# Turning the gathered slot rows with transposing transfers on SyncE's queue instead of on TensorE

## The chip, the cores and the metric

The kernel runs on one core of one Trainium2 chip. Its time is the device time of one execution in microseconds (us). Lower is better.

## What is computed

The reference is one layer of a vision tower: 32 images are cut into 36 patches each, embedded to 256 numbers, a class token is put in front (37 tokens for each image, 1184 in all), then attention with a memory, then a mixture of experts. Only the last part meets the change:

```python
shared = jnp.einsum('th,hd->td', jax.nn.silu(x_flat @ shared_w1.T), shared_w2.T)
gate_logits = x_flat @ gate_w.T
top_k_gates, top_k_idx = jax.lax.top_k(gate_logits, TOP_K)      # TOP_K = 2 of 8 experts
top_k_gates = jax.nn.softmax(top_k_gates, axis=1)
h = jnp.einsum('td,ehd->teh', x_flat, experts_w1)               # 256 -> 1024
expert_out = jnp.einsum('teh,edh->ted', jax.nn.silu(h), experts_w2)   # 1024 -> 256
selected = jnp.einsum('ted,te->td', expert_out, gates)
out = shared + selected
```

## The kernel before

The order of the work on each engine is written out by hand; semaphores tie the engines together. There are three stages.

The front (up to about 125 us) embeds, normalizes and attends, 11 tiles of 111 tokens. It writes each normalized token as a row of 512 fp16 numbers (a high and a low part of 256 numbers) to a DRAM tensor, `x_rows`.

The shared expert (about 125 to 186 us) goes over ten units of 119 tokens, `shared_up` and `shared_down`. Beside it the routing is worked out: which token goes to which slot.

The slots (from 185.7 us) are 26 tiles of 128 tokens, each of one expert. For slot j, GpSimd gathers 128 rows of `x_rows` into `slot_rows[:, j % 4]` (`gather`). TensorE turns them in four 128x128 pieces into bank 4 (`rows_of`, `turn`, L539). ScalarE copies the bank to `x_t[:, j % 2]` (`copy_x_t`, L953). Then TensorE does step j (`slot_step`): eight chunks, and in each the six matmuls of the first layer of slot j (L733, `up_chunk`) and two of the second layer of slot j - 1 (L746 and L748, `down_chunk`). After chunk 4 of step j it turns the rows of slot j + 1. Step 0 (`first_slot`) does the same with the last shared unit. ScalarE applies silu to each half of a slot (L902), VectorE makes the low part (L1238) and scales the result (L1419, L1422), and GpSimd adds the 128 result rows to the output in DRAM (L1116), one such transfer at a time.

SyncE's queue brings the weights of the experts: 36 chunks of 512 KB, `load_chunk`, L350, into a ring of six stage buffers. ScalarE and VectorE split each chunk into a high and a low half (L866, L1244). A load of chunk c waits until chunk c - 6 is split:

```python
def load_chunk(c):
    last = c - STAGES
    if last >= 0:
        wait_split(sp, last + 1)
    sp.dma_start(stage[:, c % STAGES], w_rows(c)).then_inc(stage_in[c % STAGES], 16)
```

VectorE splits chunks 18 to 21 just as step 0 begins, and two chunks in each of the steps 1 to 7 (`late_lo`). SyncE does nothing else after chunk 13: `for c in range(FRONT_CHUNKS, NCHUNK): load_chunk(c)`, with FRONT_CHUNKS = 13 and NCHUNK = 36.

## Time and profile before

| | us |
|---|---|
| median of 3 runs | 349.19 (349.02 to 349.57) |
| the profiled execution, its own time | 350.72 |
| its span | 348.8 |
| TensorE busy | 316.5 (91% of the span) |
| VectorE busy | 225.8 |
| ScalarE busy | 181.8 |
| GpSimd busy | 154.1 |

The span is the stretch from the first to the last instruction of the profiled execution. Busy time is the sum of an engine's own instructions. The stages bind differently, so the rows below are read by stage, in microseconds from the span's start.

### The profile page before, as it was taken

To read this page: it belongs to the slowest core of one execution; us is meant where nothing else is said; L and a number is where in the kernel's file an instruction comes from. 1 tells how busy PE (TensorE), PEld (TensorE's weight loads), DVE (VectorE), ACT (ScalarE), POOL (GpSimd) and SP (SyncE) were. 2 spreads that over 40 slices of the span, in tenths; PEclk is the share of its full clock that TensorE was granted. 3 is DMA by queue.
4 is the path that set the end of the run, shared out by engine and by line. 5 is a ranking of instruction groups with operands and counts; after the bars stand their busy time and mean duration, and the time that the engine had idled before them with its cause. 6 is when DMAs were issued, how large, how long until landed. Compare 5 with 4: busy or idle time off the path is not lost.

```text
span 348.8 us, 9611 instructions
## 1 busy us (share of the span) xinstructions
PE 316.5 (91%) x3366; PEld 267.9 (77%) x3366; DVE 225.8 (65%) x510; ACT 181.8 (52%) x395; POOL 154.1 (44%) x224
## 2 busy tenths in 40 slices
PE   3789899999998989999999999999999999999960
PEld 2668788877787889899999777777787777777750
DVE  0235678889888677569988687765656555554540
ACT  1136557877677575655767878763233232323210
POOL 0525557667774341510153235455435353543321
PEclk9989999999999899999999999999999999999995
DMA  7461235437300000293379878333232332323121
GB/s 260 144 212 41 99 104 157 128 114 271 106 20 26 17 25 29 59 333 90 78 179 246 311 192 251 61 60 55 44 62 36 58 46 49 48 46 48 17 32 15
DMA packets 18324, 36.36 MB, mean 104 GB/s; under 512 B 3269, under 2 KB 10920, under 8 KB 18280
## 3 DMA queue, kind: packets, MB, share of 16 engines
q1 hardware_dynamic: 11848, 27.71, 24.5%
q0 software_dynamic: 6432, 8.03, 14.7%
q8 instruction: 31, 0.51, 0.6%
q14 instruction: 13, 0.11, 0.1%
HBM read 28.52 MB, written 7.21 MB: 102 GB/s over the span
## 4 chain that ended last, share of the span: by engine, by line
PE 74%; DVE 10%; ACT 5%; issue 4%; DMA 2%; POOL 2%; SPq 0%; DVEq 0%; ACTq 0%; POOLq 0%
PE bank L733 20%; PE bank L746 14%; PE bank L460 8%; PE bank L748 6%; PE bank L485 6%; PE bank L591 6%; PE bank L550 5%; DVE weights L1244 2%; PE bank L539 2%; PE bank L493 1%; PE bank L417 1%; DMA weights<-in_w_embed 1%; DVE weights L1185 1%; DMA out_rows<-y,add_id 1%; PE bank L437 1%
## 5 line engine op out<-in xcount | busy, mean ns | idle before, releaser
L733 PEld LDWEIGHTS bank<-x_t,weights 128*128 x1248 | 87.2, 98 | 25.7
L733 PE MATMUL bank<-x_t,weights 128*128 128x128 f16 x1248 | 103.4, 219 | 0.0
L902 ACT ACTIVATE act_out<-bank 128x512 f32<-128x512 f32 (+2 forms) x72 | 42.1, 585 | 88.4 <-PE bank L733 74.9
L746 PE MATMUL bank<-weights,hid_hi 128*128 x200 | 76.1, 382 | 0.3
L1116 POOL DMA_INDIRECT out_rows<-y,add_id x26 | 42.6, 1637 | 71.0 <-DVE y L1422 53.8
L1238 DVE SCALAR_TENSOR_TENSOR hid_lo<-act_out,hid_hi 128x512 f16<-128x512 f32 (+2 forms) x72 | 48.6, 680 | 13.9 <-ACT hid_hi L913 12.5
L748 PE MATMUL bank<-weights,hid_lo 128*128 x200 | 54.5, 273 | 0.0
L1244 DVE SCALAR_TENSOR_TENSOR weights<-stage,weights 128x1024 f16<-128x1024 f32 x36 | 42.7, 1221 | 0.4 <-ACT weights L866 0.2
L460 PE MATMUL bank<-weights 128*111 128x256 f32 x132 | 32.5, 399 | 7.2 <-DMA weights<-in_w_embed 5.7
L866 ACT ACTIVATE weights<-stage 128x1024 f16<-128x1024 f32 x36 | 36.2, 1047 | 0.0
L460 PEld LDWEIGHTS bank<-weights 128*111 128x111 f32 x132 | 23.6, 184 | 13.3 <-DMA weights<-in_w_embed 5.7
L1083 POOL DMA_INDIRECT slot_rows<-x_rows,gather_id x26 | 27.3, 1051 | 13.2 <-DMA out_rows<-y 5.5
L1043 POOL TENSOR_SCALAR weights<-weights 111x1 f32<-111x1 f32 x22 | 6.4, 292 | 55.9 <-DVE weights L1142 55.8
L1419 DVE TENSOR_SCALAR y<-bank,slot_gate 128x256 f32<-128x256 f32 x25 | 12.1, 482 | 26.1 <-PE bank L748 24.6
L550 PE MATMUL bank<-x_t,weights 128*128 128x119 f16 (+1 forms) x480 | 27.6, 216 | 0.0
L591 PE MATMUL bank<-weights,hid_hi 128*119 128x256 f16 (+1 forms) x160 | 27.3, 273 | 0.2 <-DVE hid_lo L1238 0.2
L550 PEld LDWEIGHTS bank<-x_t,weights 128*128 128x128 f16 x480 | 26.2, 98 | 0.2
L1236 DVE TENSOR_SCALAR hid_hi<-act_out 128x512 f16<-128x512 f32 x36 | 15.4, 426 | 16.7 <-ACT act_out L902 14.6
L485 PEld LDWEIGHTS bank<-weights 128*128 128x128 f32 x176 | 23.7, 212 | 1.4 <-ACT weights L820 0.6
L485 PE MATMUL bank<-weights 128*128 128x111 f32 x176 | 24.4, 298 | 0.4 <-ACT weights L820 0.4
L1102 POOL DMA_DIRECT2D out_rows<-y x10 | 8.9, 890 | 33.7 <-DVE y L1436 28.9
L746 PEld LDWEIGHTS bank<-weights,hid_hi 128*128 128x128 f16 x200 | 19.3, 96 | 5.2 <-issue 1.4
(138 smaller groups left out, 544.8 us busy)
## 6 DMA issues: line engine op xcount, KB each, us to landing
stage<-in_w_ffn SPq DMA_DIRECT2D x36, 512.0 KB
weights<-in_patches SPq DMA_DIRECT2D x11, 333.0 KB, 3.0
x_rows<-rows SPq DMA_DIRECT2D x11, 111.0 KB
out_rows<-weights SPq DMA_DIRECT2D x10, 111.0 KB
out_rows<-y POOLq DMA_DIRECT2D x9, 119.0 KB, 6.1
weights<-in_w_embed SPq DMA_DIRECT2D x1, 768.0 KB, 4.4
weights<-in_w_qk SPq DMA_DIRECT2D x1, 512.0 KB, 6.2
slot_rows<-x_rows,gather_id POOLq DMA_INDIRECT x26, 3.8
```

The costliest lines, as they stand in the source:

```text
L460: mm = nc.tensor.matmul(embed_bank(t), s_patch[:, t % 2, k], s_we[:, k], start=(k == 0), stop=(k == PC - 1))
L485: mm = nc.tensor.matmul(bank[5][:, o * T:(o + 1) * T], s_wqk[:, k, o], xln_t[:, t % 2, k], start=(k == 0), stop=(k == KC - 1))
L550: mm = nc.tensor.matmul(o, weights[:, bass.ds(base + 2 * k * CHUNK + 2 * (col - col % D) + w * D + col % D, P)], x_of(2 * x + k), start=(k ...
L591: mm = nc.tensor.matmul(bank[down_bank(n)][0:m, 0:D], hid[:, n % 2, c * P:c * P + m], weights[:, at + w * D:at + (w + 1) * D], start=(c == ...
L733: mm = nc.tensor.matmul(o, weights[:, bass.ds(base + 2 * k * CHUNK + 2 * (col - col % D) + w * D + col % D, P)], x_t[:, b, (2 * x + k) * P ...
L746: nc.tensor.matmul(bank[5 + b][0:m, :], hid_hi[:, b, c * P:c * P + m], weights[:, bass.ds(at, 2 * D)], start=(c == 0), stop=False)
L748: mm = nc.tensor.matmul(bank[5 + b][0:m, 0:D], hid_lo[:, b, c * P:c * P + m], weights[:, bass.ds(at, D)], start=False, stop=(c == HC - 1))
L866: nc.scalar.mul(hi_of(c), staged_of(c), W_SCALE).then_inc(w_hi, 1)
L902: nc.scalar.activation(d_, s_, ACT.Silu, scale=1.0 / (X_SCALE * W_SCALE)).then_inc(hid_acted, 1)
L1116: nc.gpsimd.indirect_dma_start(out=out, out_offset=bass.IndirectOffsetOnAxis(ap=add_id[:, j:j + 1], axis=0), in_=y[:, j % 2], in_offset=No ...
L1238: nc.vector.scalar_tensor_tensor(out=four(hid_lo), in0=src, scalar=H_SCALE, in1=four(hid_hi), op0=ALU.mult, op1=ALU.subtract).then_inc(lo_ ...
L1244: nc.vector.scalar_tensor_tensor(out=lo_of(c), in0=staged_of(c), scalar=W_SCALE, in1=hi_of(c), op0=ALU.mult, op1=ALU.subtract).then_inc(w_ ...
```

## The change

The turns on TensorE (L539) and the copies on ScalarE (L953) are taken out, and bank 4 isn't used for them any more. In their place SyncE's queue carries four transposing transfers for each slot, each 128x128 fp16 from `slot_rows` to `x_t`, both in SBUF. A turn of slot j waits for the gather of slot j and, from slot 2 on, until the first layer of slot j - 2 is through, since `x_t` has two buffers. The weight transfers up to chunk 25 stand ahead of the turns of slots 0 and 1; the last ten stand two by two ahead of the turns of slots 2 to 6. TensorE waits at the head of step j for the four transfers of slot j. GpSimd's gather of slot j + 4 waits for them too, where it waited for the turn on TensorE.

```diff
+AHEAD = 26
-        x_turned = sem("x_turned")
-        x_t_ready = sem("x_t_ready")
+        x_t_in = [sem(f"x_t_in{i}") for i in range(2)]
-            for c in range(FRONT_CHUNKS, NCHUNK):
+            def turn_slot(j):
+
+                sp.wait_ge(slot_rows_in[j % 4], 16 * (j // 4 + 1))
+                if j >= 2:
+                    sp.wait_ge(hid_ready, 2 * (UNITS + j) - 2)
+                for q in range(4):
+                    sp.dma_start(x_t[:, j % 2, q * P:(q + 1) * P], slot_rows[:, j % 4, q * P:(q + 1) * P],
+                                 transpose=True).then_inc(x_t_in[j % 2], 16)
+
+            for c in range(FRONT_CHUNKS, AHEAD):
                 load_chunk(c)
+            turn_slot(0)
+            turn_slot(1)
+            for j in range(2, SLOT_TILES):
+                for c in range(AHEAD + 2 * (j - 2), min(AHEAD + 2 * (j - 1), NCHUNK)):
+                    load_chunk(c)
+                turn_slot(j)
...
             shared_down(UNITS - 2, 0)
-            rows_of(0)
             shared_down(UNITS - 2, 1)
...
-                pe.wait_ge(x_t_ready, j + 1)
+                pe.wait_ge(x_t_in[b], 4 * 16 * (j // 2 + 1))
                 for c in range(HC):
                     up_chunk(n, b, P, this_expert, c)
                     if c == 4 and j + 1 < SLOT_TILES:
-                        rows_of(j + 1)
                         know(j + 1)
...
-            def copy_x_t(j):
-                act.wait_ge(x_turned, j + 1)
-                act.wait_ge(hid_ready, 2 * (UNITS + j) - 2)
-                v_ = bank[4][:].bitcast(F16)[:, 0:4 * P]
-                nc.scalar.copy(x_t[:, j % 2], v_).then_inc(x_t_ready, 1)
...
                 if j >= 4:
-                    pool.wait_ge(x_turned, j - 3)
+                    pool.wait_ge(x_t_in[j % 2], 4 * 16 * ((j - 4) // 2 + 1))
```

SyncE's queue at its end, before. L391 and L393 store results of the front; the 23 transfers of L350 are the weight chunks 13 to 35:

```order
57 L393 DMA x_rows<-rows 111x512
58 L391 DMA out_rows<-weights 74x256
59 L393 DMA x_rows<-rows 111x512
60 L350 DMA stage<-in_w_ffn 128x1024 x23
61 L60 UNCONDITIONAL_BRANCH
```

The same queue in the changed kernel, where L402 is the transposing transfer:

```order
60 L350 DMA stage<-in_w_ffn 128x1024 x13
61 L402 DMA_TRANSPOSE x_t<-slot_rows 128x128 x8
62 L350 DMA stage<-in_w_ffn 128x1024 x2
63 L402 DMA_TRANSPOSE x_t<-slot_rows 128x128 x4
64 L350 DMA stage<-in_w_ffn 128x1024 x2
65 L402 DMA_TRANSPOSE x_t<-slot_rows 128x128 x4
66 L350 DMA stage<-in_w_ffn 128x1024 x2
67 L402 DMA_TRANSPOSE x_t<-slot_rows 128x128 x4
68 L350 DMA stage<-in_w_ffn 128x1024 x2
69 L402 DMA_TRANSPOSE x_t<-slot_rows 128x128 x4
70 L350 DMA stage<-in_w_ffn 128x1024 x2
71 L402 DMA_TRANSPOSE x_t<-slot_rows 128x128 x80
```

So the turns of the first two slots stand behind thirteen weight chunks (13 to 25), and 104 transfers have joined the queue.

TensorE before, at the end of the last-but-one shared unit (L591 is its second layer) and the start of step 0 (L709 reads an expert's number, the ISA rows set addresses):

```order
304 L591 MATMUL bank<-weights,hid_hi 119x256 x2
305 L591 MATMUL bank<-weights,hid_lo 119x256
306 L539 MATMUL bank<-id,slot_rows 128x128 x4
307 L591 MATMUL bank<-weights,hid_hi 119x256 x2
308 L591 MATMUL bank<-weights,hid_lo 119x256
...
315 L709 TENSOR_LOAD expert_of x2
316 L733 ISA
317 L733 MATMUL bank<-x_t,weights 128x128 x2
```

The same place of the changed kernel, where L591 has become L599 and L733 has become L734:

```order
310 L599 MATMUL bank<-weights,hid_hi 119x256 x2
311 L599 MATMUL bank<-weights,hid_lo 119x256
312 L599 MATMUL bank<-weights,hid_hi 119x256 x2
313 L599 MATMUL bank<-weights,hid_lo 119x256
314 L717 TENSOR_LOAD expert_of x2
315 L734 ISA
316 L734 MATMUL bank<-x_t,weights 128x128 x2
```

The four turning matmuls are gone here, as they are in each step, and step 0 follows directly on the shared unit; its first instruction now waits on SyncE's transfers.

## Rows read from the trace of the kernel before

**Rows 1.** The page: busy time by engine, and the chain that ended last by engine.
```profile
PE 316.5 (91%) x3366; PEld 267.9 (77%) x3366; DVE 225.8 (65%) x510; ACT 181.8 (52%) x395; POOL 154.1 (44%) x224
PE 74%; DVE 10%; ACT 5%; issue 4%; DMA 2%; POOL 2%; SPq 0%; DVEq 0%; ACTq 0%; POOLq 0%
```

**Rows 2.** Windows: stretch, then busy us and instructions by engine, PEclk, DMA share, GB/s.
```profile
200.00:232.00 32.00, 31.76 (x377) 24.69 (x376) 25.26 (x35) 25.51 (x39) 14.98 (x12) 1.00 0.57 147
232.00:330.00 98.00, 98.00 (x1180) 77.61 (x1178) 54.12 (x106) 31.34 (x53) 44.06 (x35) 1.00 0.31 48
```

**Rows 3.** Waits from 186 to 332 us: who waited for whom, us, times, longest.
```profile
ACT act_out L902 <- PE bank L733: 70.2, 44, 2.4
```

**Rows 4.** TensorE's timeline in the late steps: start us, us, line, output and input.
```profile
280.18 0.50 PE L733 MATMUL bank<-x_t,weights 128*128 128x128 f16 x6
280.51 0.39 PE L539 MATMUL bank<-id,slot_rows 128*128 128x128 f16 x4
...
281.17 0.50 PE L733 MATMUL bank<-x_t,weights 128*128 128x128 f16 x6
...
282.49 0.50 PE L733 MATMUL bank<-x_t,weights 128*128 128x128 f16 x6
...
283.15 0.50 PE L733 MATMUL bank<-x_t,weights 128*128 128x128 f16 x6
...
286.19 0.39 PE L539 MATMUL bank<-id,slot_rows 128*128 128x128 f16 x4
```

**Rows 5.** TensorE's timeline at the first matmuls of step 0.
```profile
185.73 0.33 PE L733 MATMUL bank<-x_t,weights 128*128 128x128 f16 x3
```

**Rows 6.** SyncE's queue: issues of the weight chunks 24, 25, 30 and 31.
```profile
187.59 0.33 SPq L350 DMA_DIRECT2D stage<-in_w_ffn  x1
...
188.73 0.33 SPq L350 DMA_DIRECT2D stage<-in_w_ffn  x1
...
200.62 0.33 SPq L350 DMA_DIRECT2D stage<-in_w_ffn  x1
...
201.75 0.33 SPq L350 DMA_DIRECT2D stage<-in_w_ffn  x1
```

**Rows 7.** VectorE's timeline: the low halves of chunks 18 to 21.
```profile
186.35 4.62 DVE L1244 SCALAR_TENSOR_TENSOR weights<-stage,weights 128x1024 f16<-128x1024 f32 x4
```

**Rows 8.** Windows around the start of step 0, columns as in the second group.
```profile
188.00:200.00 12.00, 11.96 (x148) 9.78 (x146) 8.96 (x11) 9.37 (x14) 2.01 (x2) 1.00 0.94 294
188.00:193.00 5.00, 4.96 (x68) 4.47 (x66) 4.46 (x6) 3.63 (x6) 0.46 (x1) 1.00 0.94 248
```

**Rows 9.** DMA issues: count, KB each, median us from issue to landing.
```profile
stage<-in_w_ffn SPq DMA_DIRECT2D x36, 512.0 KB
...
slot_rows<-x_rows,gather_id POOLq DMA_INDIRECT x26, 3.8
out_rows<-y,add_id POOLq DMA_INDIRECT x26, 3.8
...
out_rows<-y SPq DMA_DIRECT2D x1, 128.0 KB, 2.3
```

**Rows 10.** Windows near the start and at the end, where TensorE has been idle.
```profile
16.00:18.00 2.00, 2.00 (x12) 2.00 (x11) 0.00 (x0) 0.60 (x1) 0.81 (x2) 0.50 0.45 107
...
338.00:340.00 2.00, 0.00 (x0) 0.00 (x0) 0.17 (x1) 0.00 (x0) 0.50 (x1) 1.00 0.09 12
340.00:349.00 9.00, 0.00 (x0) 0.00 (x0) 0.00 (x0) 0.00 (x0) 1.05 (x1) 0.50 0.14 15
```

**Rows 11.** The chain: the same 20 matmuls of a tile at half clock and later.
```profile
15.28 3.30 PE bank L485 x16
18.57 1.25 PE bank L493 x4
...
27.95 1.77 PE bank L485 x16
29.71 0.88 PE bank L493 x4
```

**Rows 12.** GpSimd's timeline: gathers and adds of slots.
```profile
205.05 1.00 POOL L1083 DMA_INDIRECT slot_rows<-x_rows,gather_id  x1 [0.30 <-issue]
208.99 1.60 POOL L1116 DMA_INDIRECT out_rows<-y,add_id  x1 [2.94 <-DMA out_rows<-y,add_id]
...
215.00 1.58 POOL L1116 DMA_INDIRECT out_rows<-y,add_id  x1 [3.12 <-DMA out_rows<-y,add_id]
...
235.91 1.58 POOL L1116 DMA_INDIRECT out_rows<-y,add_id  x1 [1.61 <-DVE y L1422]
...
240.46 1.58 POOL L1116 DMA_INDIRECT out_rows<-y,add_id  x1 [1.67 <-DMA out_rows<-y,add_id]
```

**Rows 13.** ScalarE's timeline: silu of the second half of slots 1, 2 and 3.
```profile
197.12 0.60 ACT L902 ACTIVATE act_out<-bank 128x512 f32<-128x512 f32 x1 [1.20 <-PE bank L733]
...
203.01 0.60 ACT L902 ACTIVATE act_out<-bank 128x512 f32<-128x512 f32 x1 [1.12 <-PE bank L733]
...
208.83 0.60 ACT L902 ACTIVATE act_out<-bank 128x512 f32<-128x512 f32 x1 [1.05 <-PE bank L733]
```

More of the change, by code:

```diff
@@ L534, in logits @@
                 mm.then_inc(logits_ready, 1)
-            def turn(src):
-                for q in range(4):
-                    mm = nc.tensor.transpose(bank[4][:].bitcast(F16)[:, q * P:(q + 1) * P],
-                                             src[:, q * P:(q + 1) * P], id16[:])
-                mm.then_inc(x_turned, 1)
             def up_half(n, half_, m, base, x_of):
@@ L712, in know @@
                                                       "expert_of is written")[1][0]
-            def rows_of(j):
-                pe.wait_ge(slot_rows_in[j % 4], 16 * (j // 4 + 1))
-                if j == 0:
-                    pe.wait_ge(h2_ready, NT)
-                turn(slot_rows[:, j % 4])
             shared_down(UNITS - 2, 0)
-            rows_of(0)
             shared_down(UNITS - 2, 1)
@@ L756, in first_slot @@
                 n = UNITS
-                pe.wait_ge(x_t_ready, 1)
+                pe.wait_ge(x_t_in[0], 4 * 16)
                 for c in range(HC):
                     up_chunk(n, 0, P, base_of[0], c)
-                    if c == 5:
-                        rows_of(1)
                     if c % 4 == 0:
@@ L788, in last_slot @@
                 n, b = UNITS + j, j % 2
-                pe.wait_ge(x_t_ready, j + 1)
+                pe.wait_ge(x_t_in[b], 4 * 16 * (j // 2 + 1))
                 for c in range(HC):
@@ L1012, in _ @@
                     late_hi(n)
-            copy_x_t(0)
             late_hi(UNITS - 1)
@@ L1019, in _ @@
                     hidden_hi(UNITS + j, 0)
-                copy_x_t(j + 1)
                 silu_half(UNITS + j, P, 1)
```

## Prediction

> **What bounds the kernel now.** I read the busy times first, to see which engine could bound: TensorE, busy 91% of the span and 74% of the chain that ended last [rows 1]. An average hides stages, so the windows come next. From 200 to 330 us, where the slots are, TensorE is busy 31.76 of 32 us and 98.00 of 98 us, at full clock (PEclk 1.00), while the DMA engines are at 0.57 and 0.31 [rows 2]. The waits show the other side of it: ScalarE waited 70.2 us in the slot stage for TensorE's first layer and TensorE for nobody worth naming [rows 3]. So in the slots any time taken off TensorE's own row of matmuls is gained, and any wait put at the head of a step is paid in full.
>
> TensorE's timeline of a late step gives the size of a step. From turn to turn it is 286.19 - 280.51 = 5.68 us. The chunk with the turn takes 281.17 - 280.18 = 0.99 us, one without 283.15 - 282.49 = 0.66 us, so a turn (four matmuls, L539) costs 0.33 us of TensorE [rows 4]. Without it a step is 5.35 us.
>
> **The change, part by part.**
>
> *Turns and copies removed.* 26 turns and 26 copies go. The turn of slot 0 lies before step 0, and what it gives is swallowed by the wait below; the other 25 give 25 x 0.33 = -8.25 us. The copies on ScalarE give nothing: that engine waits for TensorE anyway [rows 3].
>
> *Where the first turns stand.* This is the term that decides. SyncE issues the transfers of slot 0 only after the load of chunk 25, and that load waits until chunk 19 is split. In the trace chunks 24 and 25 are issued at 187.59 and 188.73 us [rows 6], because VectorE splits chunks 18 to 21 in one stretch from 186.35 us [rows 7]. TensorE wants slot 0 at 185.73 us [rows 5]. Nothing in the change moves these splits forward by more than the 0.3 us of the removed turn. So the first transposing transfer is issued at 188.73 + 0.33 = 189.1 us, 3.3 us after TensorE stands waiting for it. Behind the waiting instruction on TensorE stands all of steps 0 to 25 and the last shared unit.
>
> The DMA engines are full then: share 0.94 from 188 to 200 us, 294 GB/s, that is 3.53 MB [rows 8]. In that stretch chunks 26 to 29 (4 x 0.52 MB = 2.1 MB [rows 9]) and the last parts of the shared adds (some 0.3 MB) move. What is left, about 1.1 MB, is chunks 24 and 25. At 188 us they still lie ahead nearly whole; at 248 GB/s over 188 to 193 us (1.24 MB [rows 8]) they are through at about 193.0 us. The transfers of slot 0 lie behind them on the same queue. To that I add the 2.3 us to landing of SyncE's only other transfer out of SBUF, 128 KB [rows 9]: slot 0 is ready at 195.3 us. The wait is 195.3 - 185.73 = +9.6 us. Lower bound: the transfers overtake the weights, and land 3 x 0.33 + 2.3 = 3.3 us after 189.1, at 192.4 us: +6.7 us. Upper bound, by the gathers' 3.8 us to landing and 1.0 us of issue each [rows 9, 12]: 193.0 + 3 x 1.0 + 3.8 = 199.8 us: +14.1 us.
>
> *Clock after that wait.* At the end TensorE has no matmul from 338 us on; its clock is still 1.00 in the window to 340 us and 0.50, the 1.2 GHz level, in the nine us after it. Near the start, from 16 us, it works at 0.50 [rows 10], and there the same twenty matmuls take 3.30 + 1.25 us instead of 1.77 + 0.88 [rows 11]: +1.9 us. A wait of 9.6 us is long enough for the clock to fall, by the end of the kernel. I take +1.9 us; bounds 0 and 3.8 (twice that).
>
> *The later turns, weights gone.* The turn of slot j can begin when the first layer of slot j - 2 is through. That is the end of the eighth chunk's L733, 282.49 + 0.50 = 282.99 us, 0.16 us before the next step begins at 283.15 [rows 4]. It has to be done one step later: 5.35 + 0.16 = 5.5 us are there. I call L the time from that release to the landing of the fourth transfer. If L is over 5.5 us, step j and step j - 2 form a loop and each step costs (L - 5.5)/2 more, 24 times (slots 2 to 25). The trace has no transposing transfer. Lower bound 3.3 us (above); upper bound 3 x 1.0 + 3.8 = 6.8 us by the gathers, which are small-row transfers like these [rows 9, 12]: 24 x 0.65 = +15.6 us. I take L = 4.5 us, nearer to the lower end, since the queue and the fp16 tile are SyncE's and nothing has to be generated row by row on GpSimd. It is hidden by the step: 0. If that cover goes, each us over 5.5 costs 12 us.
>
> The Trainium skill, VectorE: DVE Perf Modes, The three transpose paths, gives 1309 ns for a 128x128 bf16 transpose by DMA and 390 ns on TensorE. Its DMA figure, four times one behind another, would be an estimate of 5.2 us and, with the first issue ahead, just about L = 5.5: still nearly nothing, but no cover left. The Trainium skill, Advanced Engine Details and Errata, X-Bar Transpose (TRN2), says that such transfers are as fast as regular ones, which would leave L at the lower bound. No row here shows either.
>
> *The turns among the weights.* In before, chunks 30 and 31 are issued 3.5 and 4.6 us after the end of step 1 (197.1 us [rows 6, 13]) and need 1.05 MB / 300 GB/s = 3.5 us on top of about 1 us; they are through at about 205.2 us, 2.2 us after the end of step 2 at 203.0 us [rows 13]. The turns of slots 3 to 6 are issued behind such a pair. L is 4.5 + 2.2 = 6.7 us there, (6.7 - 5.5)/2 = 0.6 us for each of four steps: +2.4 us. The gather of slot 5 is issued at 205.05 us and lands 3.8 us later, at 208.9 us, just when its turn could begin (end of step 3, 208.8 us [rows 12, 13]). With adds 6.0 us apart here (208.99 and 215.00 us [rows 12]) against steps of 5.5, slots 5 to 8 lose some tenths: +0.6 us. Together +3.0 us; bounds 0 (L = 3.3 us) and 7 (L = 6.8 + 2.2 = 9.0 us).
>
> *Issues on SyncE.* 104 more, each some 0.33 us if like a load [rows 6]: 1.3 us of a step of 5.35 on a queue that has little else to do there. Counted in L. The weight loads behind a turn wait for a split that comes later than the turn's release, so they aren't late.
>
> **The sum.** -8.25 + 9.6 + 1.9 + 0 + 3.0 = +6.25 us. On the profiled execution (350.72 us, span 348.8) that is 357.0 us; on the median of the runs, which is 1.5 us under it, 349.19 + 6.25 = **355.4 us**.
>
> **Rivals.**
>
> *The transfers don't fit into a step* (L over 5.5 us, chance 0.30). For it: small rows on shared DMA engines, 3.8 us to landing for one gather. Against it: the DMA share is only 0.31 [rows 2]. L = 6 to 7 us gives +6 to +18 us on the sum, and the first wait grows with it: 361 to 376 us.
>
> *Slightly faster* (chance 0.07). The mechanism is the first wait alone: slot 0's transfers don't lie behind chunks 24 and 25 but overtake them, and land at 192.4 us. With no cost of the clock and none among the weights the sum is -8.25 + 6.7 = -1.6: 347.6 us. It turns at a landing of slot 0 at 194.0 us if nothing else costs anything, at 192.1 us if the clock falls. For it: nothing in the trace shows the order in which two transfers of one queue land; against it: both are on one queue, and the issue itself is 3.3 us late.
>
> *The adds become the bound* (chance 0.07). One add waits for the one before; the fastest pair in the trace is 240.46 - 235.91 = 4.55 us apart [rows 12], 0.8 us under the new step. If 104 more transfers slow their landing by 1.5 us, VectorE and so TensorE lose 0.7 us in some 17 steps, +12 us: 367 us. Against it: the share of 0.31 leaves room.
>
> **How the numbers follow.** The forecast, wait at step 0 and hidden afterwards, has a chance of 0.52 and its own range is 350.5 to 360 us (first wait 6.7 to 14.1 us, the others between their bounds). With the rivals' 0.30, 0.07 and 0.07 and 0.04 for a sum near zero, 8 times in 10 it lies from 350.5 to 372 us. A difference of 0.2% (0.7 us) is about what can be told from none. Faster 0.07, within 0.04, slower 0.89.
>
> **What the changed profile would show.** No L539 or L953 and steps of 5.35 us from 240 us on, or longer with TensorE waiting for a DMA at each head of a step: that decides the second rival. A TensorE gap of some 9 us before the first L734, released by the transfer of slot 0, with PEclk 0.5 for some us after it. The first transposing transfer issued at about 189 us. Short waits in steps 3 to 8. I am wrong if the gap is under 7 us, if the transfers take more than a step, or if they hold the SyncE queue longer than a load does.

## The result and the profile after

The changed kernel takes 388.94 us in the median (386.57 to 393.02, four runs); the kernel before, run again beside it, 349.38 us (349.02 to 351.16). The ratio is 1.1098, interval 1.1021 to 1.1175: 11% slower, some 39 us. The prediction was 355.4 us with a range of 350.5 to 372.0. The sign was right and the size was not; the time lies outside the range, and beyond its rival "the transfers don't fit into a step" too. Medians here and below are over all executions, while ratios and their intervals leave out the few that came out some us longer at a lower granted clock (one of the changed kernel's, two each of e1's and e4's, one of e12's; e1's trace is of such an execution).

The profiled execution has 386.57 us and a span of 384.7 us, against 350.72 and 348.8 us before: +35.9 us. (The medians are 39.6 us apart; the trace of before is of an execution above its median, that of the changed kernel of the fastest.) The page first, as in [rows 1]: busy times, then the chain that ended last by engine, then one of the costliest groups.

```profile
PE 321.7 (84%) x3262; PEld 262.9 (68%) x3262; DVE 226.6 (59%) x510; ACT 167.8 (44%) x369; POOL 154.0 (40%) x224
...
PE 47%; SPq 16%; DMA 12%; DVE 10%; issue 6%; ACT 5%; POOL 2%; DVEq 0%; ACTq 0%; POOLq 0%
...
L734 PE MATMUL bank<-x_t,weights 128*128 128x128 f16 x1248 | 108.8, 222 | 26.7 <-DMA x_t<-slot_rows 26.6
```

TensorE has 104 matmuls fewer and its share of the chain fell from 74% to 47%. What came in is SyncE's queue (SPq, 16%, 0% before) and the DMA (12%, 2% before): the chain now runs through the issue and the landing of transfers. The waits say the same:

```profile
PE bank L734 <- DMA x_t<-slot_rows: 26.6, 20, 9.9
```

The columns are us in total, times and the longest. TensorE, which hardly waited in the slots of before [rows 2], waits for a transfer at the head of 20 steps.

**Where the 35.9 us lie.** ScalarE's silu of the second half of a slot marks the steps. Slots 0, 8 and 25 in the kernel before:

```profile
191.15 0.60 ACT L902 ACTIVATE act_out<-bank 128x512 f32<-128x512 f32 x1 [0.74 <-PE bank L733]
...
237.89 0.60 ACT L902 ACTIVATE act_out<-bank 128x512 f32<-128x512 f32 x1 [1.54 <-PE bank L733]
...
334.15 0.60 ACT L902 ACTIVATE act_out<-bank 128x512 f32<-128x512 f32 x1 [1.54 <-PE bank L733]
```

and in the changed one:

```profile
201.36 0.60 ACT L900 ACTIVATE act_out<-bank 128x512 f32<-128x512 f32 x1 [1.39 <-PE bank L734]
...
256.85 0.60 ACT L900 ACTIVATE act_out<-bank 128x512 f32<-128x512 f32 x1 [2.31 <-PE bank L734]
...
370.06 0.60 ACT L900 ACTIVATE act_out<-bank 128x512 f32<-128x512 f32 x1 [1.39 <-PE bank L734]
```

| stretch | before | after | more |
|---|---|---|---|
| to the end of step 0 | 191.15 | 201.36 | 10.2 |
| slots 1 to 8, beside the last weights | 46.74 | 55.49 | 8.8 |
| slots 9 to 25, weights gone | 96.26 (5.66 a step) | 113.21 (6.66 a step) | 17.0 |

The second and the third stretch are called "the loaded part" and "the late part" in every run below.

**The start of step 0.** TensorE's timeline, which answers to [rows 5]:

```profile
184.35 0.27 PE L599 MATMUL bank<-weights,hid_lo 128*119 128x256 f16 x1
194.55 0.82 PE L734 MATMUL bank<-x_t,weights 128*128 128x128 f16 x6 [9.93 <-DMA x_t<-slot_rows]
...
195.81 0.85 PE L734 MATMUL bank<-x_t,weights 128*128 128x128 f16 x6
...
197.09 0.85 PE L734 MATMUL bank<-x_t,weights 128*128 128x128 f16 x6
...
198.18 0.50 PE L734 MATMUL bank<-x_t,weights 128*128 128x128 f16 x6
```

A wait of 9.93 us, and then chunks 1.26, 1.28 and 1.09 us apart where a chunk took 0.66 us [rows 4]. The windows have the reason in their PEclk column: 1.00 before the wait, half of it (the 1.2 GHz level) from 188 to 198 us, and 1.00 again. Their last two columns (DMA share, GB/s) show the weight chunks 24 and 25 going through until about 192.5 us:

```profile
188.00:190.00 2.00, 0.00 (x0) 0.00 (x0) 1.69 (x2) 0.00 (x0) 0.00 (x0) 0.50 0.84 205
190.00:192.00 2.00, 0.00 (x0) 0.00 (x0) 0.00 (x0) 0.00 (x0) 0.00 (x0) 0.50 0.99 352
192.00:194.00 2.00, 0.00 (x0) 0.00 (x0) 0.00 (x0) 0.00 (x0) 0.00 (x0) 0.50 0.32 79
...
196.00:198.00 2.00, 2.00 (x18) 1.94 (x16) 0.00 (x0) 0.00 (x0) 0.00 (x0) 0.51 0.10 19
198.00:200.00 2.00, 2.00 (x29) 1.97 (x28) 0.00 (x0) 1.23 (x2) 0.00 (x0) 1.00 0.46 72
```

SyncE's queue (start, us, line, count) shows what was late:

```profile
181.27 6.51 SPq L350 DMA_DIRECT2D stage<-in_w_ffn  x4
187.83 10.10 SPq L402 DMA_TRANSPOSE x_t<-slot_rows  x8
197.98 1.05 SPq L350 DMA_DIRECT2D stage<-in_w_ffn  x2
201.43 5.89 SPq L402 DMA_TRANSPOSE x_t<-slot_rows  x4
```

The first transposing transfer is issued at 187.83 us, 3.2 us after TensorE ran dry (194.55 - 9.93 = 184.62 us). And the eight transfers of slots 0 and 1 hold the queue for 10.10 us. That is no wait: the source view of L402 gives the duration of each issue, least, median and greatest in ns:

```profile
L402 SPq DMA_TRANSPOSE x_t<-slot_rows x104: 1093/1232/2318, 187.8 to 361.8; - x104
```

An issue takes 1.23 us in the median, not the 0.33 us of a weight load [rows 6]. The loads behind them, chunks 26 and 27, have to wait until 197.98 us; before, the six loads from 187.59 us on (chunks 24 to 29) were all issued by 196.1 us.

**The loaded part.** TensorE waits for a transfer at the head of six of the steps 1 to 8, 7.0 us in all. The longest is at the head of step 5:

```profile
230.53 0.67 PE L734 MATMUL bank<-x_t,weights 128*128 128x128 f16 x6 [2.30 <-DMA x_t<-slot_rows]
...
232.00:233.00 1.00, 1.00 (x10) 0.85 (x8) 1.00 (x2) 0.00 (x0) 0.00 (x0) 0.55 1.75 266
```

The first line is of the timeline, the second a window: the granted clock falls here too, behind a wait of only 2.30 us, and the next chunks take some 1.3 us more. The turn of that slot needed 8.5 us from its release (221.60 us) to its landing (230.06 us); its issues stand right behind a pair of weight loads. The weights themselves were not late: ScalarE, which splits them, never waited for a chunk in the slots.

**A late step.** One piece of the chain from 289 to 297 us, the turn of slot 15: the release by TensorE's end of slot 13's first layer (L400 is SyncE's wait), four issues one behind another, the landing of the last, and TensorE's first matmul:

```profile
289.38 0.02 SPq L400
289.39 0.03 issue
289.42 1.09 SPq L402
290.52 0.04 issue
290.56 1.23 SPq L402
291.79 0.04 issue
291.83 1.24 SPq L402
293.07 0.04 issue
293.11 3.55 DMA x_t<-slot_rows
296.66 0.13 issue
296.79 0.23 PE bank L734
```

From release to landing it is 296.66 - 289.38 = 7.3 us. The DMA row counts from the start of the last issue: 3.55 us to landing, of which 1.23 us are the issue. The 2.3 us of SyncE's transfer out of SBUF in [rows 9] count from the start of its issue too, so the landing is 1.25 us longer than that one. This release-to-landing is what the prediction called L and took as 4.5 us.

### The profile page after: what moved, and what is told of

Same layout as the page of the kernel before. It is cut to its first block, busy times and chain, and to the rows that moved or that the text cites. A ratio compares the mean times of both kernels' runs of the same rounds, so it can differ in the third digit from the quotient of the medians.

```text
span 384.7 us, 9478 instructions
## 1 busy us (share of the span) xinstructions
PE 321.7 (84%) x3262; PEld 262.9 (68%) x3262; DVE 226.6 (59%) x510; ACT 167.8 (44%) x369; POOL 154.0 (40%) x224
## 4 chain that ended last, share of the span: by engine, by line
PE 47%; SPq 16%; DMA 12%; DVE 10%; issue 6%; ACT 5%; POOL 2%; DVEq 0%; ACTq 0%; POOLq 0%
SPq L402 15%; DMA x_t<-slot_rows 10%; PE bank L734 10%; PE bank L475 8%; PE bank L747 6%; PE bank L599 6%; PE bank L558 5%; PE bank L500 4%; DVE weights L1234 3%; PE bank L749 3%; DMA weights<-in_w_embed 1%; PE bank L508 1%; PE bank L432 1%; DVE weights L1175 1%; DMA out_rows<-y,add_id 1%
## 5 line engine op out<-in xcount | busy, mean ns | idle before, releaser
L734 PE MATMUL bank<-x_t,weights 128*128 128x128 f16 x1248 | 108.8, 222 | 26.7 <-DMA x_t<-slot_rows 26.6
L734 PEld LDWEIGHTS bank<-x_t,weights 128*128 x1248 | 88.7, 99 | 60.8 <-issue 35.9
L475 PE MATMUL bank<-weights 128*111 128x256 f32 x132 | 33.4, 407 | 7.2 <-DMA weights<-in_w_embed 5.6
L1226 DVE TENSOR_SCALAR hid_hi<-act_out 128x512 f16<-128x512 f32 x36 | 15.8, 439 | 33.2 <-ACT act_out L900 23.0
L599 PE MATMUL bank<-weights,hid_hi 128*119 128x256 f16 (+1 forms) x160 | 27.9, 278 | 0.2 <-DVE hid_lo L1228 0.2
L500 PEld LDWEIGHTS bank<-weights 128*128 128x128 f32 x176 | 21.7, 196 | 1.4 <-ACT weights L818 0.6
L500 PE MATMUL bank<-weights 128*128 128x111 f32 x176 | 22.2, 281 | 0.4 <-ACT weights L818 0.4
```

Source lines behind the costliest of these rows:

```text
L475: mm = nc.tensor.matmul(embed_bank(t), s_patch[:, t % 2, k], s_we[:, k], start=(k == 0), stop=(k == PC - 1))
L500: mm = nc.tensor.matmul(bank[5][:, o * T:(o + 1) * T], s_wqk[:, k, o], xln_t[:, t % 2, k], start=(k == 0), stop=(k == KC - 1))
L599: mm = nc.tensor.matmul(bank[down_bank(n)][0:m, 0:D], hid[:, n % 2, c * P:c * P + m], weights[:, at + w * D:at + (w + 1) * D], start=(c == ...
L734: mm = nc.tensor.matmul(o, weights[:, bass.ds(base + 2 * k * CHUNK + 2 * (col - col % D) + w * D + col % D, P)], x_t[:, b, (2 * x + k) * P ...
```

## The experiments

The stretches are those of the table above; a "late step" is the late part over 17. Where a run has a ratio, its interval stands behind it.

### What an issue costs: e1 and e2

e1 turns a slot with one transfer of the same 128 KB instead of four (semaphore counts follow):

```diff
-                for q in range(4):
-                    sp.dma_start(x_t[:, j % 2, q * P:(q + 1) * P], slot_rows[:, j % 4, q * P:(q + 1) * P],
-                                 transpose=True).then_inc(x_t_in[j % 2], 16)
+                sp.dma_start(x_t[:, j % 2].rearrange("p (q c) -> p q c", c=P), slot_rows[:, j % 4],
+                             transpose=True).then_inc(x_t_in[j % 2], 16)
```

> The changed kernel, but one transposing transfer of 128x512 for each slot instead of four of 128x128. Theory A (SyncE's sequencer pays some 1.2 us for each transposing instruction, 4.9 us of the 7.2 us from release to landing): one issue takes 1.2 to 2 us, release to landing falls to about 4 to 4.5 us, under the 5.5 us that a step hides, steps go from 6.66 to about 5.35 to 5.5 us and the first wait shrinks by some 2 us: 353 to 359 us. Theory B (the sequencer pays by the amount turned, not by the instruction): the one issue takes about 4.9 us and the time stays at 385 to 390 us. Theory C (the data's way through the DMA engines and its landing is the cost): also 385 to 390 us, with a short issue and a long landing.

Measured: 364.78 us beside 350.28, ratio 1.0331 (1.028 to 1.0382), above the 353 to 359 us expected. The issues and the waits:

```profile
L401 SPq DMA_TRANSPOSE x_t<-slot_rows x26: 1189/1191/2045, 189.2 to 337.4; - x26
...
PE bank L733 <- DMA x_t<-slot_rows: 13.1, 3, 11.0
```

A transfer four times the size is issued in 1.19 us, no more than the small one's 1.23: the price is per instruction. Waits at the heads of steps went from 20 to 3, and the late part from 113.21 to 96.13 us. So the loss of 17 us among the late steps was the four issues in a row. The loaded part, with the order of the queue as in the change, is 48.18 us instead of 55.49, so most of the 8.8 us lost there goes with the number of issues too. But a late step is 96.13 / 17 = 5.65 us now, not 5.35: though nothing waits for a transfer, the turns that are gone gave nothing. That needed an explanation of its own (next section but one).

e2 leaves `transpose=True` away, so it copies the rows and leaves out the turn; four transfers a slot as in the change.

```diff
                 for q in range(4):
-                    sp.dma_start(x_t[:, j % 2, q * P:(q + 1) * P], slot_rows[:, j % 4, q * P:(q + 1) * P],
-                                 transpose=True).then_inc(x_t_in[j % 2], 16)
+                    sp.dma_start(x_t[:, j % 2, q * P:(q + 1) * P], slot_rows[:, j % 4, q * P:(q + 1) * P]).then_inc(x_t_in[j % 2], 16)
```

> The changed kernel with plain copies of the same four 128x128 pieces in place of the transposing transfers; it leaves out the turn itself, so the first layer multiplies unturned rows. Theories A and B (issue of the transposing form on SyncE): an issue falls from 1.23 to about 0.3 to 0.4 us, release to landing to about 3.6 us, steps to 5.35 us, 353 to 358 us. Theory C (data movement of small rows between SBUF and SBUF beside the gathers and adds): the copies land as late as the turns did, 380 us or more.

Measured: 363.62 us, ratio 1.0375 (1.0335 to 1.0415), above the 353 to 358 us expected.

```profile
L402 SPq DMA_DIRECT2D x_t<-slot_rows x104: 464/601/1367, 188.3 to 337.4; - x104
...
PE bank L733 <- DMA x_t<-slot_rows: 11.3, 2, 10.1
```

A plain copy of the same piece is issued in 0.60 us, half the time; four of them fit into a step (late part 96.74 us). The slow issue belongs to the transposing instruction. The wait at step 0 stays, 10.1 us here and 11.0 us in e1. The chain shows how in e1: its first transfer needs 7.57 us from issue to landing.

```profile
189.16 7.57 DMA x_t<-slot_rows
```

It was issued behind the loads of chunks 24 and 25, on the same queue. (In e5 below, with the same transfers, it took 6.96 us and the wait was 10.4 us.)

### What the issues do to others: e3 and e4

e3 is the kernel before, which turns on TensorE, with the 104 transposing transfers at the places of the change, but into a buffer that nobody reads. The gather of slot j + 4 waits for them too (left out of the lines below, like the semaphores of the buffer).

```diff
+                for q in range(4):
+                    sp.dma_start(rows[:, j % 2, q * P:(q + 1) * P], slot_rows[:, j % 4, q * P:(q + 1) * P],
+                                 transpose=True).then_inc(spare_in[j % 2], 16)
...
-            for c in range(FRONT_CHUNKS, NCHUNK):
+            for c in range(FRONT_CHUNKS, 26):
                 load_chunk(c)
+            turn_slot(0)
+            turn_slot(1)
+            for j in range(2, SLOT_TILES):
+                for c in range(26 + 2 * (j - 2), min(26 + 2 * (j - 1), NCHUNK)):
+                    load_chunk(c)
+                turn_slot(j)
```

> The kernel before, with its turns on TensorE, and in addition all 104 transposing transfers at the places they have in the changed kernel, into a tile that nobody reads. Theory A or B (only the wait of TensorE for them costs): within 1 us of before, 348.5 to 351 us. Rival (the transfers slow gathers, adds or weights on the shared DMA engines, or TensorE's and VectorE's access to SBUF): over 355 us, with longer waits for the adds. A part between would be the share of weight loads that stand behind the slow issues: at most 1 to 3 us.

Measured: 355.39 us, ratio 1.0163 (1.0127 to 1.0199): 5 us for transfers that nobody reads, more than was expected, and just what the rival had (over 355 us). The late part is as before (95.85 us against 96.26); the whole loss lies in the loaded part, 52.37 us against 46.74. One line of SyncE's queue and two of the waits:

```profile
226.59 1.05 SPq L351 DMA_DIRECT2D stage<-in_w_ffn  x2
...
ACT weights L887 <- DMA stage<-in_w_ffn: 8.7, 9, 3.0
...
PE bank L754 <- ACT x_t L974: 3.7, 3, 2.7
```

The last pair of weight chunks is issued at 226.59 us; before, the fourteen loads from chunk 22 on were all issued by 214.4 us. ScalarE waits nine times for a chunk, which it never did before, and so TensorE waits for ScalarE's copies. Steps 5 to 7 take 6.58, 8.81 and 7.09 us where they took 5.8. So the weights come late, and each turn puts four issues of 1.23 us ahead of the next two loads. That the issues alone did it is not shown: the transfers also fill the DMA engines (from 204 to 208 us a share of 1.07 at 147 GB/s, against 0.74 at 198 GB/s before), and the waits for landed adds grew (GpSimd's from 14.3 to 17.6 us, VectorE's from 1.4 to 8.4 us between 186 and 332 us).

e4 gives the changed kernel a third turned buffer, in memory that the front has done with, so that a turn may begin a step earlier.

```diff
+        x_of_slot = [x_t[:, 0], x_t[:, 1], rows[:, 0]]
...
-                if j >= 2:
-                    sp.wait_ge(hid_ready, 2 * (UNITS + j) - 2)
+                if j == 2:
+                    sp.wait_ge(hid_ready, 2 * UNITS - 4)
+                if j >= 3:
+                    sp.wait_ge(hid_ready, 2 * (UNITS + j) - 4)
                 for q in range(4):
-                    sp.dma_start(x_t[:, j % 2, q * P:(q + 1) * P], slot_rows[:, j % 4, q * P:(q + 1) * P],
-                                 transpose=True).then_inc(x_t_in[j % 2], 16)
+                    sp.dma_start(x_of_slot[j % 3][:, q * P:(q + 1) * P], slot_rows[:, j % 4, q * P:(q + 1) * P],
+                                 transpose=True).then_inc(x_t_in[j % 3], 16)
...
```

> The changed kernel with a third buffer for the turned rows (the tile of the front's rows is used again), so that a turn may begin one step earlier. Theory A or B (time from release to landing of 7.2 us against 5.5 us; SyncE is busy 4.9 us of a step, which still fits): steps fall to 5.35 to 5.5 us, and 24 x 1.2 us go: 356 to 361 us. Rival (SyncE's or the DMA engines' throughput, not the time to landing, sets the pitch of 6.66 us): under 8 us gained, 380 us or more.

Measured: 370.12 us (365.88 to 372.15) against 350.28, with no interval on record. The late part is 96.32 us: the loop between step j and step j - 2 was the cause of the 17 us, and with two steps of room L of 7.3 us is hidden. But the total missed the expectation of 356 to 361 us, in three places: the late steps come down only to 5.67 us, as in e1; the first wait is 10.95 us; and the loaded part is 52.47 us. That this is close to e3's 52.37 us is chance, for ScalarE waits for no weight chunk here. The chain goes through an add that took 7.23 us to land, the gather behind it (6.04 us) and the turn behind that, and TensorE waits 5.2 us for turned rows, in three steps.

### Why the turns gave nothing: e5 to e8

With the waits for transfers gone, the late step without its turn stayed at 5.65 to 5.69 us (e1, e2, e4). TensorE's timeline of e1 at chunk 4 shows what stands there:

```profile
289.44 0.50 PE L733 MATMUL bank<-x_t,weights 128*128 128x128 f16 x6
290.10 0.39 PE L746 MATMUL bank<-weights,hid_hi 128*128 x1 [0.16 <-issue]
290.32 0.27 PE L748 MATMUL bank<-weights,hid_lo 128*128 x1
290.43 0.50 PE L733 MATMUL bank<-x_t,weights 128*128 128x128 f16 x6
```

290.43 - 289.44 = 0.99 us, as with the turn in [rows 4], and an idle piece "issue". In the code `know(j + 1)` stands right behind the turn: TensorE reads the next expert's number (L709, a register load). The theory: this read, not the four matmuls, is what chunk 4 pays; the turn only covered it. e5 is e1 with all 26 reads ahead of step 0:

```diff
-            know(0)
-            know(1)
+            for j in range(SLOT_TILES):
+                know(j)
...
-                    if c == 4 and j + 1 < SLOT_TILES:
-                        know(j + 1)
```

> One 128x512 transposing transfer for each slot, and all 26 expert numbers read by TensorE's sequencer once before step 0 instead of one in each step after chunk 4. Theory D (in the kernel before, the four turning matmuls covered the read of the next expert's number; with the turn gone TensorE stands still for the same 0.33 us, which is why steps stayed at 5.63 us): late steps fall from 5.63 to about 5.3 us, 24 x 0.3 = 7 us less than with the reads in the steps: 355 to 358 us. Rival E (late steps of 5.63 us are set by the chain of adds on GpSimd or by VectorE): no change, 361 to 365 us.

Measured: 358.10 us beside 350.3, ratio 1.0228 (1.0181 to 1.0275), where e1 had 1.0331; 355 to 358 us were expected. The reads in a row cost nothing extra here, because TensorE waits for slot 0 meanwhile. The late part is 90.83 us, 5.34 a step; L733 of chunk 4 and of its neighbours follow each other every 0.66 us:

```profile
288.88 0.50 PE L733 MATMUL bank<-x_t,weights 128*128 128x128 f16 x6
...
289.54 0.50 PE L733 MATMUL bank<-x_t,weights 128*128 128x128 f16 x6
```

e6 undoes the change where it hurts and keeps it where it should pay: TensorE turns slots 0 to 7, and one transfer a slot turns 8 to 25, behind the last weight load (BY_DMA = 8).

```diff
             for c in range(FRONT_CHUNKS, NCHUNK):
                 load_chunk(c)
+            for j in range(BY_DMA, SLOT_TILES):
+                sp.wait_ge(slot_rows_in[j % 4], 16 * (j // 4 + 1))
+                sp.wait_ge(hid_ready, 2 * (UNITS + j) - 2)
+                sp.dma_start(x_t[:, j % 2].rearrange("p (q c) -> p q c", c=P), slot_rows[:, j % 4],
+                             transpose=True).then_inc(x_t_in[j % 2], 16)
...
-                        rows_of(j + 1)
+                        if j + 1 < BY_DMA:
+                            rows_of(j + 1)
...
```

> The kernel before with its turns on TensorE up to slot 7 and one 128x512 transposing transfer for each of the slots 8 to 25, all behind the last weight chunk; expert numbers read in each step as before. Both the first wait and the turns among the weights are gone, and a transfer lands within the 5.5 us that a step hides. Theory D: late steps stay at 5.63 to 5.66 us and the time is that of the kernel before, within 0.7 us. My own step of the prediction (a turn costs TensorE 0.33 us that its removal gives back): 18 x 0.33 = 6 us less, 344 us.

Measured: 350.39 us beside 350.3, ratio 1.0002 (0.9986 to 1.0018), late part 96.14 us. TensorE waits for no transfer in it, and still 18 turns taken off TensorE are worth nothing. The prediction's 0.33 us each is refuted by this run alone.

e7 is e6 with the reads ahead of step 0 as in e5, e8 the kernel before with them.

> As the run with late transfers (TensorE turns slots 0 to 7, one transfer each for 8 to 25), and all expert numbers read before step 0. Theory D: late steps of 5.3 us, 18 x 0.3 = 5 to 6 us less than the kernel before: 343.5 to 346 us. Rival E (adds or VectorE set the late step): the time of the kernel before, 349 to 351 us.

> The kernel before, all turns on TensorE, with all expert numbers read before step 0. Theory D, if turn and read lie fully beside each other: steps stay at 5.65 us, since the turn alone fills the 0.33 us: within 0.7 us of before. If the read had cost something beside the turn, the steps from slot 1 on get shorter by up to 0.2 us: 345 to 348 us.

| run | reads in the steps | turns in the late steps | late part | median | ratio |
|---|---|---|---|---|---|
| before | yes | yes | 96.26 | 350.3 | |
| e6 | yes | no | 96.14 | 350.39 | 1.0002 (0.9986 to 1.0018) |
| e8 | no | yes | 93.99 | 357.52 | 1.0208 (1.018 to 1.0235) |
| e7 | no | no | 92.16 | 354.84 | 1.0123 (1.0092 to 1.0155) |

The late part answers as expected; the medians don't (343.5 to 346 us were expected for e7, at most some 350 for e8). The 26 reads in a row are paid somewhere else, at the head of step 0 (e8):

```profile
194.52 0.82 PE L733 MATMUL bank<-x_t,weights 128*128 128x128 f16 x6 [8.57 <-issue]
```

8.57 us for 26 reads is 0.33 us each, and the clock falls on top, as in the changed kernel. That a read costs as much when it stands bare among other reads had not been allowed for.

### The reads spread out: e9 and e10

So the reads were laid singly between matmuls of the shared units 5 to 9, one after every second chunk, in the kernel of e6 (e9) and in the kernel before (e10).

```diff
+            def read_some():
+                place[0] += 1
+                if place[0] % 2 == 0 and place[1] < SLOT_TILES:
+                    if place[1] == 0:
+                        pe.wait_ge(experts_known, 1)
+                    know(place[1])
+                    place[1] += 1
...
+                    if n >= 7:
+                        read_some()
...
+                elif 5 <= n < UNITS - 1:
+                    read_some()
```

> TensorE turns slots 0 to 7, one 128x512 transfer turns each of the slots 8 to 25, and the 26 reads of expert numbers are spread, one for each 6 to 12 matmuls, over the last shared units (from about 166 us on). If the sequencer is far enough ahead there, the reads cost nothing and the late steps are 5.29 us, the earlier ones 5.5 to 5.7: 350.3 - 18 x 0.36 - 7 x 0.15 = 342.8 us, 342 to 344.5. If each read stops TensorE for some 0.3 us there too (as the 26 in a row did, 8.6 us), they give the gain back: 349 to 352 us.

> The kernel before, all turns on TensorE, with the 26 reads spread over the last shared units. Late steps were 5.50 us with the reads taken out of them and the turns left in: 350.3 - 25 x 0.15 = 346.5 us, 346 to 348, if the reads are hidden in the shared units; 353 to 356 us if each costs its 0.3 us there.

Measured, beside 350.0: e9 342.32 us, ratio 0.9775 (0.9747 to 0.9803); e10 346.08 us, ratio 0.9892 (0.9862 to 0.9921). Both as expected, and both faster than the kernel before. e9's windows, over the stretch with the reads and over the late steps:

```profile
166.00:186.00 20.00, 20.00 (x276) 19.80 (x275) 17.57 (x28) 14.58 (x22) 8.97 (x8) 1.00 0.61 153
240.00:320.00 80.00, 80.00 (x966) 63.88 (x964) 46.86 (x91) 17.91 (x30) 40.06 (x30) 1.00 0.51 74
```

TensorE is busy in the whole of both, and slot 0 ends at 190.63 us against 191.15: no cost of the spread reads is seen there. From the late parts each price follows, over 17 steps:

- read beside a turn, before to e10: (96.26 - 93.99) / 17 = 0.13 us
- read without a turn, e6 to e9: (96.14 - 90.94) / 17 = 0.31 us
- turn without a read, e10 to e9: (93.99 - 90.94) / 17 = 0.18 us
- turn with a read behind it, before to e6: (96.26 - 96.14) / 17 = 0.01 us

The two overlap: together they cost 0.31 us, and taking away either alone gives 0.13 us or nothing. Each late part is of one trace. Those with the same code in the late steps are 93.99 and 93.99 us (e8, e10) and 90.83, 90.94 and 92.16 us (e5, e9, e7), so a price is good to some 0.07 us, and the 0.31 us is the firm one.

### The queue's order, and whether the parts add up: e11 and e12

e11 is the changed kernel with slot 0's four transfers ahead of chunk 22 instead of behind chunk 25.

```diff
-            for c in range(FRONT_CHUNKS, AHEAD):
+            for c in range(FRONT_CHUNKS, 22):
                 load_chunk(c)
             turn_slot(0)
+            for c in range(22, AHEAD):
+                load_chunk(c)
             turn_slot(1)
```

> The changed kernel with the four transfers of slot 0 ahead of weight chunk 22 instead of behind chunk 25; nothing else moved. Theory A (issue of four at 1.2 us, then landing, and the weights in front of them): they are issued from about 182 us, as soon as the gather has landed, and slot 0 is ready near 189 us: the first wait falls from 9.9 us to 4 to 6 us. Chunks 22 to 25 are issued some 5 us later, which may cost 1 to 3 us in the steps among the weights. 389 us becomes 382 to 386 us. Rival (slot 0's gather or the engines' backlog sets the wait): under 1.5 us gained.

Measured: 383.43 us beside 350.0, ratio 1.0957 (1.0916 to 1.0997). The queue, and TensorE at step 0:

```profile
181.15 5.87 SPq L402 DMA_TRANSPOSE x_t<-slot_rows  x4
187.07 2.00 SPq L350 DMA_DIRECT2D stage<-in_w_ffn  x4
```

```profile
188.67 0.82 PE L736 MATMUL bank<-x_t,weights 128*128 128x128 f16 x6 [4.53 <-DMA x_t<-slot_rows]
```

The wait fell from 9.93 to 4.53 us; step 0 ends at 196.15 instead of 201.36. So 5 of the 10 us hang on where the transfers stand in the queue. The rest is the time of four issues and a landing even from an early place. The clock fell behind this shorter wait too (PEclk 0.50 from 187 to 193 us).

e12 is e6 with four 128x128 transfers for each of slots 8 to 25, as in the change.

```diff
-                sp.dma_start(x_t[:, j % 2].rearrange("p (q c) -> p q c", c=P), slot_rows[:, j % 4],
-                             transpose=True).then_inc(x_t_in[j % 2], 16)
+                for q in range(4):
+                    sp.dma_start(x_t[:, j % 2, q * P:(q + 1) * P], slot_rows[:, j % 4, q * P:(q + 1) * P],
+                                 transpose=True).then_inc(x_t_in[j % 2], 16)
```

> TensorE turns slots 0 to 7; slots 8 to 25 are turned by four 128x128 transfers each, as in the changed kernel, behind the last weight chunk. If the parts of the changed kernel's loss add up (10.2 us at step 0, 8.8 us in the steps among the weights, 17 us in the late steps of 6.66 instead of 5.65 us), this keeps the last part alone: 366 to 369 us. If the late steps are only slow because of what went before (adds and gathers running late), it is under 358 us.

Measured: 370.24 us, ratio 1.0561 (1.0489 to 1.0633), a little above the 366 to 369 us expected; late part 111.97 us, against 96.14 in e6. That is 15.8 us from the four issues alone, without any late start and without a weight load near. The changed kernel has 17.0 there. For step 0, 10.2 us, e11 puts 5 down to the queue's order. The 8.8 us of the loaded part are, by the changed kernel's own trace, 7.0 us of waits for turned rows and some 1.3 us of half clock in step 5.

## Why the prediction missed

Step by step, as the prediction put them.

- **What bounds the kernel** was right: TensorE's own row, and any wait at the head of a step is paid in full.
- **Turns and copies removed, 25 x 0.33 = -8.25 us: wrong, it is 0.** The 0.33 us of chunk 4 in [rows 4] were read off as the price of the four matmuls, though the read of the next expert's number stands in the same chunk. The change's own TensorE order, quoted ahead of the prediction, shows that instruction (L709, L717) left in place. e6 (ratio 1.0002), e5 and the four prices of e9 and e10 settle it. The late step of 5.35 us is right for a kernel without turn and read (e9: 90.94 / 17 = 5.35).
- **Where the first turns stand, +9.6 us: right in size, in part by luck.** The wait measured 9.93 us, and step 0 starts 8.8 us later than before. The first issue was put at 189.1 us and came at 187.83; the weights were through at about 192.5 us, predicted 193.0; the last transfer landed at 194.3 us, predicted 195.3. The path is only in part the predicted one: the four issues, taken as 0.33 us each, fill the time until 192.8 us, and the last transfer lands 2.73 us after its issue began, so hardly anything is left that the weights would have held up. Where the issues are fewer or faster the weights do hold it up: the one transfer of e1 landed 7.57 us after its issue began, the last of e2 4.59 us, and the waits were as long (11.0 and 10.1 us). Either of the two causes fills about the same time; only a place ahead of the chunks (e11, 4.53 us) shortens it.
- **Clock after that wait, +1.9 us: right in kind.** Half clock until 198 us; the first three chunks take 3.63 instead of 1.98 us, +1.65 us. Step 0 ends 10.2 us late in all, against 9.6 + 1.9 = 11.5 predicted.
- **The later turns, L = 4.5 us, cost 0: wrong, and this is the step that failed.** L is 7.3 us, over the upper bound of 6.8 too: three issues of 1.09 to 1.24 us one behind another, then 3.55 us from the start of the fourth to landing. The lower bound of 3.3 us, to which L was held near, had 3 x 0.33 + 2.3: it is short by 2.7 us on the issues and 1.25 us on the landing. The price of an issue was taken from weight loads [rows 6], a plain transfer out of DRAM, and the landing from one early store (which was not SyncE's only other transfer out of SBUF: `x_rows<-rows` is one too). The bound from the gathers, 3 x 1.0 + 3.8, was short on the issues. The formula of the loop was nearly right: (7.3 + 0.1 - 5.5) / 2 = 1.0 on 5.35 would be 6.3 us a step. Measured are 6.66 us: the bare read adds to each step, and the first chunk behind a wait takes 0.89 us instead of 0.66 (296.79 to 297.68). e12 shows the cost by itself (+15.8 us), and e1, with one issue for each slot, takes it away. The loss on 17 steps is 17.0 us; against the 17 x 0.33 us gain that was forecast that is 22.6 us of the miss.
- **The Trainium skill's figures there.** The Trainium skill, VectorE: DVE Perf Modes, The three transpose paths, has 1309 ns for a 128x128 transpose by DMA. One behind another, issue for issue, that is near what is measured (1.23 us); the prediction worked out 5.2 us from it, with no landing behind the last. Its 390 ns for TensorE is more than the 0.18 us that a removed turn of four gives here. The Trainium skill, Advanced Engine Details and Errata, X-Bar Transpose (TRN2), has such transfers as fast as regular ones. For these small pieces the runs differ: 1.23 us an issue against 0.60 us for the plain copy of the same piece (e2). The measurement decides.
- **Among the weights, +3.0 us: the mechanism was right, the size too small.** Slots 1 to 8 lost 8.8 us, against 3.0 - 8 x 0.33 = 0.4 predicted. Turns behind a pair of weight loads do come late, as it said (8.5 us for slot 5), but on top of the longer L, and the clock fall of step 5 was not in the sum. "Issues on SyncE" said that the weight loads aren't late. They are issued later, as in e3, but no engine waited for one in the changed kernel, which starts its slots 8.8 us later.
- **The range.** The prediction's own bounds don't give its 350.5 to 360 us. They give 349.19 - 8.25 + 6.7 = 347.6 us up to 349.19 - 8.25 + 14.1 + 3.8 + 7 = 365.8 us, and 381.4 us with the 15.6 us of the later turns. The measured time lies even above that, by less than the 8.25 us of gain that didn't come.
- **The rivals.** "The transfers don't fit into a step" happened, with L 0.3 us over its own 6 to 7 and without the gain it still counted. "Slightly faster" needed transfers that overtake the weight chunks; a single one issued right behind two of them took 7.57 us (e1) and 6.96 us (e5), which speaks against it. "The adds become the bound" is not seen: TensorE's waits name the transposing transfer.

Put together, the 35.9 - 6.25 = 29.6 us that the sum is short: 22.6 in the late steps, 8.4 beside the weights, and -1.3 at step 0, which is 29.7. That step 0 came out near the forecast is in part two errors that cancel.

**Left open.** No run takes the loaded part of the changed kernel apart; the reading above is from its waits. What part of e3's 5.6 us comes from the slow issues and what part from full DMA engines is open, and so is why the first chunk behind a wait takes 0.2 us more.

## What to carry to other kernels

Price a transfer by its issue first, from a row of the same kind of instruction: here the issue time multiplied by the number of instructions, delayed what stood behind it on the queue, and depended on the kind of instruction, not on the amount. Before a removed instruction is credited with the gap around it, look for what else shares that gap; here a register read lay under the turn, and only taking away both gave time. And a transfer that a step waits for belongs ahead of the bulk loads on its queue (e11), or behind the last of them, as in e9, where one transfer a slot and spread reads make a kernel 2.3% faster than before, 1.1% of it from the reads alone (e10).

## What the runs showed of the hardware

- A transposing transfer from SBUF to SBUF occupied SyncE's queue for 1.23 us in the median (1.09 to 2.32 us) when it moved 32 KB (128x128), and for 1.19 us when it moved 128 KB (128x512, e1); a plain copy of 128x128 for 0.60 us (e2), a weight load of 512 KB from DRAM for 0.33 us [rows 6].
- From the start of its issue to landing a transposing transfer of 32 KB took 3.55 us in a late step, and one of 128 KB took 7.57 us (e1) and 6.96 us (e5) right behind two weight loads.
- A register read on TensorE's sequencer cost 0.31 to 0.33 us where it stood bare (e8's 8.57 us for 26 in a row, e6 against e9), 0.13 us behind a turn, and nothing measurable when it stood alone between the matmuls of the shared units. Why it is free there and not in chunk 4 of a step was not tried.
- TensorE's granted clock went from 1.00 to 0.50 in the first wait of the slots, whether that was 9.93, 8.57 (e8) or 4.53 us long (e11), and behind a wait of 2.30 us in step 5. It came back 3 to 5.5 us after TensorE had begun to work again (3.5 us in the changed kernel, 5.5 us in e8).
